# Pair products inside groups of eight fields moved to a layout with the batch in the rows, in a DLRM interaction kernel

## Chip, cores and metric

One core of one Trainium2 chip. The metric is the time of one execution on the device in microseconds (us); lower is better. All data are 32-bit floats.

## What is computed

The reference, cut to what matters: 32 fields are looked up in 32 tables, one row of 64 numbers each for 1024 examples. For each of the 496 pairs of fields i < j a number comes out of a 64x64 matrix of that pair, and these numbers with 16 dense features go through three layers.

```python
e = stack([tbl_0[ids[:, 0]], ..., tbl_31[ids[:, 31]]], axis=1)     # 1024 x 32 x 64
iu, ju = triu_indices(32, k=1)                                     # 496 pairs
z = einsum('bpe,fpe,bpf->bp', e[:, iu], kernel, e[:, ju])
h = concatenate([z, dense_ctx], axis=1)                            # 512 columns
h = maximum(h @ W_top1 + b_top1, 0)                                # 512
h = maximum(h @ W_top2 + b_top2, 0)                                # 256
y = h @ W_top3                                                     # 1
```

## The kernel before

The batch goes through in four quarters of 256 examples (QB). Two fields make a pack, 16 packs k = 0..15. Everything is written out by hand, an instruction stream per engine with counting semaphores between them.

- **Gather** (POOL, L173): per pack and quarter four indirect DMAs bring the rows of two fields for twice 128 examples into `raw`, examples in the partitions. `raw` holds 16 packs; a place is free once its pack is transposed.
- **Pack** (`transpose_pack`, L307, and `copy_x`, L192): two transposes on TensorE put a pack into `prep_ps` with the 2 x 64 features in the partitions and 256 examples in the columns, and ScalarE copies it to `xt`. `prep_ps` is a single buffer.
- **Unit** (`transform`, L278 to L299, and `multiply`, L240 to L261): a pack k is multiplied with two earlier packs m, m+1, which is eight pairs of fields. TensorE runs four matmuls of 64 rows, 128 columns of weights and 256 examples, two at a time (L289 on rows 0 to 63, L290 on rows 64 to 127), into one of three places of `t_ps`. VectorE multiplies the 1024 columns with pack k (L252) into `prod`. For odd k one unit of the row is a special one (L295, L297; on VectorE L256, L258, L260). There are 64 units a quarter. `t_ps` has three places, so a unit waits until VectorE has read the one three before it (`take_turn`).
- **Feature sums** (`feature_sums`, L321 and L324): the sum over the 64 features of a pair is a matmul too, with 32 columns of a 0/1 selector as weights and 512 columns of products, four of them side by side in `z_ps`. A burst is four units, and the sums of a burst follow the units of the next one. There are 16 bursts and so 16 rounds of sums a quarter. L329 adds the 16 dense features to free rows of `z_ps`.
- **Layers** (`copy_z`, L199; `layer`, L343, L352, L358; `copy_layer`, L209, L212, L215): ScalarE copies `z_ps` twice a quarter, and the layers of a quarter run in four pieces inside bursts 2 to 5 of the next quarter, the last quarter's at the end. A piece takes a place of `t_ps` as a unit does.

The order on TensorE (L366 to L379) is, for each burst b: its four units, a piece of a layer, the first pack due for burst b+1, the sums of burst b-1, the other packs due. ScalarE has the same order of its copies, and each engine works strictly in its written order.

```python
for b in range(QUARTERS * NB + 1):
    ... transform(v) for the four units of b ...
    if piece_after(b): layer(*piece_after(b))
    for p in before_sums(b + 1): transpose_pack(p)
    if b: feature_sums(b - 1)
    for p in after_sums(b + 1): transpose_pack(p)
```

Of the kernel before, what the change touches and what calls it, by code (L numbers as in the profile page):

```python
# [6 lines left out]
P = 128  # L7
# [4 lines left out]
PACKS = FIELDS // 2  # L12
W = 2 * QB
ZT = 2
RAW = 16
XRING = 2 * PACKS
TRING = 3
PRING = 8
BURST = 4

UNITS = [(k, tuple(range(m, min(m + 2, k)))) for k in range(1, PACKS) for m in range(0, k, 2)]
NU = len(UNITS)
NB = NU // BURST
TILE_BURSTS = NB // ZT
PACK_COL = [P * (k * (k - 1) // 2) + EMBED * (k // 2) for k in range(PACKS + 1)]
KCOLS = PACK_COL[PACKS]


def weight_cols(k, m):

    begin = PACK_COL[k] + P * m
    return slice(begin, begin + (EMBED if m == k else P))


def burst_sums(b):

    sums = [(u, n) for u in range(b * BURST, (b + 1) * BURST) for n in range(2)]
    return sorted(sums, key=lambda un: un[1] == 1 and len(UNITS[un[0]][1]) == 1)  # L40
# [3 lines left out]
Z_SLOT = {un: (b // TILE_BURSTS, at % 4, 2 * (b % TILE_BURSTS) + at // 4)  # L44
          for b in range(NB) for at, un in enumerate(burst_sums(b))}

FREE = [Z_SLOT[u, 1] for u, (_, ms) in enumerate(UNITS) if len(ms) == 1]
FREE_GROUPS = sorted({(t, g) for t, g, _ in FREE})


def packs_due(b):

    q, at = divmod(b, NB)
    if q >= QUARTERS:
        return []
    last = UNITS[at * BURST + BURST - 1][0]
    due = [k for k in range(PACKS) if k <= last and (at == 0 or k > UNITS[at * BURST - 1][0])]
    if at == 0 and q:
        due = due[2:]
    due = [q * PACKS + k for k in due]  # L60
    if at == NB - 1 and q < QUARTERS - 1:
        due += [(q + 1) * PACKS, (q + 1) * PACKS + 1]
    return due


def before_sums(b):


    return packs_due(b)[:1] if b > NB else []


def after_sums(b):
    return packs_due(b)[len(before_sums(b)):]

PIECES = 4
PIECE_BURST = 2
# [4 lines left out]
def piece_after(b):  # L83

    q, at = divmod(b, NB)
    return (q - 1, at - PIECE_BURST) if q and 0 <= at - PIECE_BURST < PIECES else None
# [6 lines left out]

def turns():

    out = []
    for b in range(QUARTERS * NB):
        out += [("unit", b * BURST + n) for n in range(BURST)]
        if piece_after(b):
            out.append(("piece", piece_after(b)))  # L100
    return out + [("piece", (QUARTERS - 1, piece)) for piece in range(PIECES)]
# [6 lines left out]
def build(nc, ids, tables, kmat, dense, w1, b1, w2, b2, w3, sel, sel_dense, ident, y):  # L108
# [3 lines left out]
    with ctx:  # L112
# [9 lines left out]
        sel_dense_sb = sb("sel_dense_sb", [P, len(FREE_GROUPS), 32])  # L122
        w1_sb = sb("w1_sb", [P, 2 * ZT, H1])
# [4 lines left out]
        dense_sb = sb("dense_sb", [P, BATCH])  # L128
        k_sb = sb("k_sb", [P, KCOLS])
        raw = sb("raw", [P, RAW, BT, 2, EMBED])  # L130
        xt = sb("xt", [P, XRING, QB])
        prod = sb("prod", [P, PRING, 4, QB])
        zt = sb("zt", [P, ZT, W])
        h1 = sb("h1", [P, H1 // P, QB])
        h2 = sb("h2", [P, H2 // P, QB])
        y_sb = sb("y_sb", [1, BATCH])

        t_ps = ctx.enter_context(nc.psum_tensor("t_ps", [P, TRING, 4, QB], fp32))
        prep_ps = ctx.enter_context(nc.psum_tensor("prep_ps", [P, QB], fp32))
# [3 lines left out]
        k_in = [sem(f"k_in{k}") for k in range(PACKS)]  # L143
        gathered = [sem(f"gathered{s}") for s in range(RAW)]
        transposed, x_copied = sem("transposed"), sem("x_copied")
        t_done, prod_done, summed, z_copied = sem("t_done"), sem("prod_done"), sem("summed"), sem("z_copied")
        layer_done, layer_copied, y_stored = sem("layer_done"), sem("layer_copied"), sem("y_stored")

        block = ctx.enter_context(nc.Block())

        @block.sync
        def _(sp):
# [296 lines left out]
```

## Time and profile before

| | |
|---|---|
| median of 3 runs | 471.23 us (471.15 to 472.52) |
| the profiled execution's own time | 471.08 us |
| its span, first to last instruction | 469.3 us |
| TensorE matmuls busy | 438.2 us, 93% |
| VectorE busy | 305.6 us, 65% |
| POOL (gathers) busy | 241.9 us, 52% |
| ScalarE busy | 42.0 us, 9% |
| granted TensorE clock, mean | 0.996 |

How it is read: busy is the time in which an engine had an instruction at work, and the sum over engines is far over the span because they overlap. The span is 1.8 us shorter than the execution's own time. The same matmul counts twice in the profile, as two instructions. A line such as L289 is a line of the kernel; `t_ps<-xt,k_sb` names the output and the inputs; PEld is TensorE's weight load, which runs beside its matmuls.

### The profile page before, as it was taken

What the parts mean: (1) busy time and instruction counts of PE and PEld (TensorE: products, weight loads), DVE (VectorE), ACT (ScalarE), POOL (GpSimd) and SP (SyncE); (2) the same over time, 40 slices, a digit from 0 to 9 for tenths busy, and PEclk for the clock granted to TensorE, in tenths of its full rate; (3) what the DMA queues carried; (4) which work ended last, traced back from release to release, by engine and by line L of the source; (5) the groups of instructions that cost most, each with busy time, mean ns of one, the idle gap of its engine ahead of it and who ended that gap; (6) DMA issues with size and microseconds to landing.
All of it is one profiled execution on the core that took longest, in us unless ns stands there. A gap on an engine that the chain in (4) does not pass through costs nothing.

```text
span 469.3 us, 7916 instructions
## 1 busy us (share of the span) xinstructions
PE 438.2 (93%) x3432; PEld 263.1 (56%) x3432; DVE 305.6 (65%) x320; ACT 42.0 (9%) x101; POOL 241.9 (52%) x260
## 2 busy tenths in 40 slices
PE   0159999999999999999999999999999999999988
PEld 0036556556456765665556674565556765565646
DVE  0045878788774656788777456788787437878850
ACT  1000000100111110000011110000001110000002
POOL 5777777777777777777777777753300000000000
PEclk9998999999999999999999999999999999999999
DMA  4444454511111111111111111110000000000000
GB/s 125 110 114 135 134 168 154 162 28 27 27 27 28 27 27 29 27 26 30 27 30 25 27 29 27 27 22 13 11 3 0 1 1 0 1 1 1 0 1 0
DMA packets 11834, 19.41 MB, mean 41 GB/s; under 512 B 5141, under 2 KB 5785, under 8 KB 11673
## 3 DMA queue, kind: packets, MB, share of 16 engines
q0 software_dynamic: 8192, 8.40, 10.1%
q1 hardware_dynamic: 2592, 8.34, 5.6%
q10 hardware_dynamic: 1016, 2.17, 1.3%
q8 instruction: 27, 0.44, 0.4%
q14 instruction: 7, 0.05, 0.0%
HBM read 18.89 MB, written 0.00 MB: 40 GB/s over the span
## 4 chain that ended last, share of the span: by engine, by line
PE 91%; POOL 5%; issue 2%; DMA 1%; DVE 1%; ACT 0%; DVEq 0%
PE t_ps L289 46%; PE z_ps L321 23%; PE t_ps L343 6%; POOL raw L173 5%; PE prep_ps L307 4%; PE t_ps L295 3%; PE t_ps L352 3%; PE t_ps L290 1%; PE z_ps L324 1%; PE t_ps L358 1%; DVE prod L252 1%; DMA raw<-tbl,ids_sb 1%; PE z_ps L329 1%; DMA ids_sb<-ids 1%; ACT xt L192 0%
## 5 line engine op out<-in xcount | busy, mean ns | idle before, releaser
L252 DVE TENSOR_TENSOR prod<-t_ps,xt 128x1024 f32<-128x1024 f32 x224 | 259.1, 1215 | 93.1 <-PE t_ps L290 93.1
L173 POOL DMA_INDIRECT raw<-tbl,ids_sb x256 | 241.7, 944 | 93.7 <-issue 76.2
L289 PE MATMUL t_ps<-xt,k_sb 64*128 64x256 f32 x960 | 232.4, 390 | 0.0
L290 PE MATMUL t_ps<-xt,k_sb 64*128 64x256 f32 x960 | 232.4, 390 | 0.0
L289 PEld LDWEIGHTS t_ps<-xt,k_sb 64*128 64x128 f32 x960 | 172.3, 188 | 67.7 <-issue 26.6
L290 PEld LDWEIGHTS t_ps<-xt,k_sb 64*128 64x128 f32 x960 | 172.4, 189 | 0.0
L321 PE MATMUL z_ps<-prod,sel_sb 128*32 128x512 f32 x960 | 122.9, 599 | 0.5 <-DVE prod L260 0.5
L321 PEld LDWEIGHTS z_ps<-prod,sel_sb 128*32 128x32 f32 x960 | 26.3, 109 | 54.7 <-issue 46.5
L256 DVE TENSOR_TENSOR prod<-t_ps,xt 128x512 f32<-128x512 f32 x32 | 21.9, 685 | 53.2 <-PE t_ps L297 53.2
L307 PE MATMUL prep_ps<-ident_sb,raw 128*128 128x128 f32 x128 | 28.5, 305 | 27.8 <-DMA raw<-tbl,ids_sb 26.7
L192 ACT ACTIVATE xt<-prep_ps 128x256 f32<-128x256 f32 x64 | 24.5, 382 | 284.6 <-PE prep_ps L307 283.3
L307 PEld LDWEIGHTS prep_ps<-ident_sb,raw 128*128 128x128 f32 x128 | 13.9, 144 | 55.1 <-issue 35.9
L343 PE MATMUL t_ps<-zt,w_sb 128*128 128x256 f32 x128 | 29.5, 385 | 0.8 <-ACT zt L199 0.8
L343 PEld LDWEIGHTS t_ps<-zt,w_sb 128*128 128x128 f32 x128 | 23.8, 190 | 6.6 <-DVE prod L252 2.4
L295 PE MATMUL t_ps<-xt,k_sb 64*64 64x256 f32 x64 | 21.1, 410 | 0.0
L297 PE MATMUL t_ps<-xt,k_sb 64*64 64x256 f32 x64 | 21.0, 410 | 0.0
L324 PE MATMUL z_ps<-prod,sel_sb 128*32 128x256 f32 x64 | 16.7, 379 | 0.0
L352 PE MATMUL t_ps<-h,w_sb 128*128 128x256 f32 x64 | 14.8, 384 | 0.0
L258 DVE TENSOR_TENSOR prod<-t_ps,xt 64x256 f32<-64x256 f32 x32 | 13.7, 427 | 0.4
L260 DVE TENSOR_TENSOR prod<-t_ps,xt 64x256 f32<-64x256 f32 x32 | 13.3, 417 | 0.4
L352 PEld LDWEIGHTS t_ps<-h,w_sb 128*128 128x128 f32 x64 | 11.9, 190 | 2.6 <-DVE prod L252 1.1
L209 ACT ACTIVATE h<-t_ps,b_sb 128x256 f32<-128x256 f32 x16 | 7.6, 473 | 57.2 <-PE t_ps L343 57.2
(15 smaller groups left out, 42.0 us busy)
## 6 DMA issues: line engine op xcount, KB each, us to landing
raw<-tbl,ids_sb POOLq DMA_INDIRECT x256, 2.5
w_sb<-w ACTq DMA_DIRECT2D x1, 1024.0 KB
k_sb<-kmat SPq DMA_DIRECT2D x1, 992.0 KB, 5.0
k_sb<-kmat SPq DMA_DIRECT2D x1, 896.0 KB
k_sb<-kmat SPq DMA_DIRECT2D x1, 864.0 KB, 4.5
k_sb<-kmat SPq DMA_DIRECT2D x1, 768.0 KB, 4.2
k_sb<-kmat SPq DMA_DIRECT2D x1, 736.0 KB, 4.0
k_sb<-kmat SPq DMA_DIRECT2D x1, 640.0 KB, 3.9
```

The costliest lines, as they stand in the source:

```text
L173: nc.gpsimd.indirect_dma_start(raw[:, p % RAW, t, f, :], None, tables[2 * k + f], bass.IndirectOffsetOnAxis(ap=ids_sb[:, q * BT + t, 2 * k ...
L192: nc.scalar.activation(xt[:, p % XRING, :], prep_ps[:], ACT.Copy).then_inc(x_copied, 1)
L252: nc.vector.tensor_tensor(prod[:, own], t_ps[:, slot], xt[:, here:here + 1, :].broadcast_to([P, 4, QB]), ALU.mult).then_inc(prod_done, 1)
L256: nc.vector.tensor_tensor(prod[:, own, 0:4:2, :], t_ps[:, slot, 0:4:2, :], xt[:, here:here + 1, :].broadcast_to([P, 2, QB]), ALU.mult)
L289: nc.tensor.matmul(t_ps[:, slot, i, :], k_sb[0:EMBED, cols], xt[0:EMBED, x, :], start=True, stop=True)
L290: last = nc.tensor.matmul(t_ps[:, slot, 2 + i, :], k_sb[EMBED:P, cols], xt[EMBED:P, x, :], start=True, stop=True)
L295: nc.tensor.matmul(t_ps[EMBED:P, slot, 1, :], k_sb[0:EMBED, cols], xt[0:EMBED, xa, :], start=True, stop=True)
L307: last = nc.tensor.transpose(prep_ps[:, t * P:(t + 1) * P], raw[:, p % RAW, t, :, :], ident_sb[:])
L321: last = nc.tensor.matmul(z_ps[rows, :], weights, prod[:, own, 2 * n:2 * n + 2, :], start=(pos == 0), stop=(pos == 15 and (tile, group) no ...
L324: last = nc.tensor.matmul(z_ps[rows, 0:QB], weights, prod[:, own, 2, :], start=False, stop=False)
L343: last = nc.tensor.matmul(t_ps[:, slot, 2 * n, :], w1_sb[:, t, m * P:(m + 1) * P], zt[:, t // 2, t % 2 * QB:(t % 2 + 1) * QB], start=(t == ...
L352: last = nc.tensor.matmul(t_ps[:, slot, 2 * n, :], w2_sb[:, t, n * P:(n + 1) * P], h1[:, t, :], start=(t == 0), stop=(t == H1 // P - 1))
```

## The change

The 16 packs are put into four groups g of four packs (eight fields). Pairs of fields from different groups stay as they are: F units, now 48 a quarter, 12 rounds of four. The 28 pairs inside a group go another way, in B units: the transposed features of a pack are now the weights and the 64x64 matrices move (`batch_transform`), so that the product has 128 examples in the partitions and the features in the columns. VectorE multiplies it with the gathered rows in `raw` as they lie (`batch_multiply`, two instructions), and ScalarE sums each pair's 64 columns with one activation that has an accumulator output (`sum_along`). A group takes four B units: two halves t of 128 examples, and for each a part 0 of 16 pairs and a part 1 of 12 pairs. So there are 64 units a quarter as before, 48 F and 16 B.

- ScalarE gets 28 activations of 128x64 per group and half, 896 in all. Their results lie in `zb`, example by row; two transposes a quarter (`turn_sums`) and a copy (`copy_turned`) turn them into the fourth part of the first layer's input. The dense features are loaded straight into `zb`, and L329 with its weights is gone.
- The order: in quarter 0 the B units stand in rounds 0, 2, 3, 6, 7 and 11; in quarters 1 and 2 a group's four stand ahead of the four F units of every third round (eight units in a row); in quarter 3 two B units stand among the four F units of rounds 0 to 7.
- From the second quarter on, packs are transposed two at a time into a `prep_ps` of 512 columns, and copied with one activation. From quarter 2 on a pair is made one round earlier.
- `raw` holds six groups, free once the group's last B unit is multiplied; `prod_a` holds six B units.
- In the last quarter three of the four parts of the first layer run ahead of the last feature sums (`last_layers`).

The numbers of rounds below run on over the quarters (12 is the first of quarter 1). Its core:

```diff
+F_UNITS = [(k, (m, m + 1)) for k in range(GROUP, PACKS) for m in range(0, k // GROUP * GROUP, 2)]
+B_UNITS = [(g, t, part) for g in range(GROUPS) for t in range(BT) for part in range(2)]
+def batch_units(r):
+    q, at = divmod(r, ROUNDS)
+    if q == 0:
+        begin = {0: (0, 4), 2: (4, 6), 3: (6, 8), 6: (8, 10), 7: (10, 12), 11: (12, 16)}.get(at, (0, 0))
+    elif q < QUARTERS - 1:
+        begin = (NBU // GROUPS * (at // 3), NBU // GROUPS * (at // 3 + (at % 3 == 0)))
+    else:
+        begin = (min(NBU, 2 * at), min(NBU, 2 * at + 2))
+    return [("B", q, u) for u in range(*begin)]
+def sums_after(r):
+    if r < EARLY_ROUNDS:
+        return []
+    if r < ROUNDS:
+        return [(0, u) for u in {10: (), 11: (12, 13)}.get(r, (r + 2,))]
+    own = [(q, u) for kind, q, u in ORDER[r] if kind == "B"]
+    return [(0, 14), (0, 15)] + own if r == ROUNDS else own
+def fills_due(r):
+    return [j for j, packs in enumerate(FILLS)
+            if FIRST_ROUND[j] - (packs[0] >= 2 * PACKS) == r and r >= EARLY_ROUNDS]
+def before_sums(r):
+    return fills_due(r)[:1] if r > 4 else []
+def after_sums(r):
+    return fills_due(r)[len(before_sums(r)):]
...
+            def sum_along(q, u):
+                g, t, part = B_UNITS[u]
+                own = nth(q, u) % ARING
+                act.wait_ge(prod_done, COUNT["B", q, u])
+                col = g * GROUP_SUMS + part * 2 * SUMS[0]
+                for n in range(2):
+                    for f in range(SUMS[part]):
+                        cells = prod_a[:, own, n, f * EMBED:(f + 1) * EMBED]
+                        last = nc.scalar.activation(cells, cells, ACT.Copy, accum_out=zb[:, q, t, col:col + 1])
+                        col += 1
+                last.then_inc(reduced, 1)
...
+            for r in range(LAST):
+                if r < EARLY_ROUNDS:
+                    for unit in ORDER[r]:
+                        for j in fills_before(unit):
+                            copy_fill(j)
+                            if j >= GROUP:
+                                sum_along(0, j - GROUP)
+                if piece_after(r):
+                    copy_layer(*piece_after(r))
+                if turn_after(r) is not None:
+                    copy_turned(turn_after(r))
+                for j in before_sums(r + 1):
+                    copy_fill(j)
+                if r and r % ROUNDS in (0, WHOLE):
+                    copy_z(*((r // ROUNDS, 0) if r % ROUNDS else (r // ROUNDS - 1, 1)))
+                for j in after_sums(r + 1):
+                    copy_fill(j)
+                if r == ROUNDS // 2:
                     load_weights()
+                for q, u in sums_after(r):
+                    sum_along(q, u)
...
+            def batch_multiply(q, u):
...
+                if nth(q, u) >= ARING:
+                    dve.wait_ge(reduced, nth(q, u) - ARING + 1)
+                dve.wait_ge(t_done, COUNT["B", q, u])
...
+                if part == 0:
+                    against_first(0, 2 * EMBED)
+                    against_first(2 * EMBED, 6 * EMBED).then_inc(prod_done, 1)
...
+            def batch_transform(q, u):
+                g, t, part = B_UNITS[u]
+                product = t_ps[:, take_turn(TURN_OF["B", q, u])].rearrange("p (n h) w -> p n (h w)", n=2)
+                pe.wait_ge(prep_copied, pack_copied(q, GROUP * g + GROUP - 1))
...
+                if part == 0:
+                    for pack, begin in ((1, 0), (3, 2 * EMBED)):
+                        for n in range(2):
+                            last = against_first(n, pack, begin)
+                else:
+                    for n in range(2):
+                        against_first(n, 2, 0)
+                    for c in range(2):
+                        for n in range(2):
+                            last = within(n, c)
+                last.then_inc(t_done, 1)
...
+            for r in range(LAST):
+                for unit in ORDER[r]:
...
+                if piece_after(r):
+                    layer(*piece_after(r))
+                if turn_after(r) is not None:
+                    turn_sums(turn_after(r))
+                for j in before_sums(r + 1):
+                    transpose_fill(j)
...
+                if r:
+                    feature_sums(r - 1)
+                for j in after_sums(r + 1):
+                    transpose_fill(j)
+            last_layers(QUARTERS - 1)
```

In `batch_transform` the 64-row matmuls move 128 and 384 columns (part 0) or 256 and twice 64 columns (part 1), each on either half of the rows. On VectorE part 0 is an instruction of 2 x 128 and one of 2 x 384 columns, part 1 one of 2 x 256 and one of 4 x 64.

## Rows read from the trace of the kernel before

**Rows 1.** The page: busy time of each engine, and TensorE's in 40 slices.

```profile
PE 438.2 (93%) x3432; PEld 263.1 (56%) x3432; DVE 305.6 (65%) x320; ACT 42.0 (9%) x101; POOL 241.9 (52%) x260
...
PE   0159999999999999999999999999999999999988
```

**Rows 2.** The page's chain that ended last, shares by line.

```profile
PE t_ps L289 46%; PE z_ps L321 23%; PE t_ps L343 6%; POOL raw L173 5%; PE prep_ps L307 4%; PE t_ps L295 3%; PE t_ps L352 3%; PE t_ps L290 1%; PE z_ps L324 1%; PE t_ps L358 1%; DVE prod L252 1%; DMA raw<-tbl,ids_sb 1%; PE z_ps L329 1%; DMA ids_sb<-ids 1%; ACT xt L192 0%
```

**Rows 3.** Stretches of the span, columns in the first line.

```profile
core 0: us, PE busy (x) PEld busy (x) DVE busy (x) ACT busy (x) POOL busy (x), PEclk, DMA share, GB/s
...
36.00:41.00 5.00, 5.00 (x33) 4.11 (x32) 2.60 (x3) 0.38 (x1) 3.78 (x5) 0.67 0.54 151
...
135.30:243.60 108.30, 108.30 (x859) 65.19 (x859) 76.31 (x81) 10.11 (x25) 81.80 (x88) 1.00 0.16 27
...
352.00:454.80 102.80, 102.23 (x816) 61.60 (x815) 71.19 (x73) 8.18 (x20) 0.00 (x0) 1.00 0.00 1
```

**Rows 4.** Timeline of TensorE's matmuls: start us, length us, line, operation.

```profile
201.19 0.48 PE L289 MATMUL t_ps<-xt,k_sb 64*128 64x256 f32 x1
...
204.85 1.92 PE L321 MATMUL z_ps<-prod,sel_sb 128*32 128x512 f32 x16
206.70 0.48 PE L289 MATMUL t_ps<-xt,k_sb 64*128 64x256 f32 x1
...
210.36 0.44 PE L307 MATMUL prep_ps<-ident_sb,raw 128*128 128x128 f32 x2
210.72 1.50 PE L321 MATMUL z_ps<-prod,sel_sb 128*32 128x512 f32 x12
```

**Rows 5.** Timeline of VectorE in the same stretch.

```profile
202.44 4.62 DVE L252 TENSOR_TENSOR prod<-t_ps,xt 128x1024 f32<-128x1024 f32 x4 [1.22 <-PE t_ps L290]
```

**Rows 6.** Timeline of TensorE at the sums that place the dense features.

```profile
303.13 0.60 PE L329 MATMUL z_ps<-dense_sb,sel_dense_sb 128*32 128x256 f32 x4
303.66 0.48 PE L289 MATMUL t_ps<-xt,k_sb 64*128 64x256 f32 x1
```

**Rows 7.** Groups by line and shape: busy us, mean ns of one, idle before.

```profile
L252 DVE TENSOR_TENSOR prod<-t_ps,xt 128x1024 f32<-128x1024 f32 x224 | 259.1, 1215 | 93.1 <-PE t_ps L290 93.1
...
L192 ACT ACTIVATE xt<-prep_ps 128x256 f32<-128x256 f32 x64 | 24.5, 382 | 284.6 <-PE prep_ps L307 283.3 <-ACT y_sb L215 1.3
...
L256 DVE TENSOR_TENSOR prod<-t_ps,xt 128x512 f32<-128x512 f32 x32 | 21.9, 685 | 53.2 <-PE t_ps L297 53.2
...
L258 DVE TENSOR_TENSOR prod<-t_ps,xt 64x256 f32<-64x256 f32 x32 | 13.7, 427 | 0.4
...
L199 ACT ACTIVATE zt<-z_ps 128x512 f32<-128x512 f32 x8 | 4.8, 597 | 36.6 <-PE z_ps L329 36.6
```

**Rows 8.** Timeline of the weight loads at a unit's start.

```profile
201.19 0.18 PEld L289 LDWEIGHTS t_ps<-xt,k_sb 64*128 64x128 f32 x1 [0.83 <-issue]
...
201.30 0.19 PEld L289 LDWEIGHTS t_ps<-xt,k_sb 64*128 64x128 f32 x1
```

**Rows 9.** Timeline of the start: the transposes of packs 0 and 3.

```profile
9.80 0.66 PE L307 MATMUL prep_ps<-ident_sb,raw 128*128 128x128 f32 x2 [9.80 <-DMA raw<-tbl,ids_sb]
...
24.80 0.69 PE L307 MATMUL prep_ps<-ident_sb,raw 128*128 128x128 f32 x2 [4.51 <-DMA raw<-tbl,ids_sb]
```

**Rows 10.** The chain of waits in order of time.

```profile
47.59 1.85 PE z_ps L321 x16
...
155.13 3.65 PE t_ps L343 x16
```

**Rows 11.** Timeline of TensorE at the last feature sums.

```profile
452.83 1.49 PE L321 MATMUL z_ps<-prod,sel_sb 128*32 128x512 f32 x11 [0.53 <-DVE prod L260]
```

**Rows 12.** Timeline of ScalarE: two operations one behind the other.

```profile
149.30 0.47 ACT L209 ACTIVATE h<-t_ps,b_sb 128x256 f32<-128x256 f32 x1 [1.19 <-PE t_ps L343]
149.67 0.38 ACT L192 ACTIVATE xt<-prep_ps 128x256 f32<-128x256 f32 x1
```

More of the change, by code:

```diff
@@ L12 @@
 PACKS = FIELDS // 2
+GROUP = 4
+GROUPS = PACKS // GROUP
+GW = 2 * GROUP * EMBED
 W = 2 * QB
-ZT = 2
-RAW = 16
+RING = 6
 XRING = 2 * PACKS
 TRING = 3
-PRING = 8
-BURST = 4
[L23 to L34, printed above, removed]
@@ new lines, in order @@
+def order():
+    out = []
+    for r in range(LAST):
+        q, at = divmod(r, ROUNDS)
+        feature = [("F", q, at * BURST + n) for n in range(BURST)]
+        batch = batch_units(r)
+        if q == 0:
+            out.append(batch + feature)
+        else:
+            out.append([x for n in range(BURST) for x in batch[n:n + 1] + feature[n:n + 1]]
+                       if q == QUARTERS - 1 else batch + feature)
+    return out
+ORDER = order()
+COUNT = {unit: n + 1 for n, unit in enumerate(x for units in ORDER for x in units)}
@@ new lines, with newest_pack, first_round @@
+QUARTER_DONE = [max(COUNT["F", q, NF - 1], COUNT["B", q, NBU - 1]) for q in range(QUARTERS)]
+def newest_pack(unit):
+    kind, q, u = unit
+    return q * PACKS + (F_UNITS[u][0] if kind == "F" else B_UNITS[u][0] * GROUP + GROUP - 1)
+FILLS = [(p,) for p in range(PACKS)] + [(p, p + 1) for p in range(PACKS, QUARTERS * PACKS, 2)]
+FILL_OF = {p: j for j, packs in enumerate(FILLS) for p in packs}
+def first_round(j):
+    return min(r for r, units in enumerate(ORDER) for x in units if newest_pack(x) >= FILLS[j][0])
@@ L94, in turns @@
+PREP_COUNT = {use: n + 1 for n, use in enumerate(prep_uses())}
 def turns():
     out = []
[L97 to L101, printed above, removed]
+    for r, units in enumerate(ORDER):
+        out += units
+        if piece_after(r):
+            out.append(("piece",) + piece_after(r))
+    return out + [("piece", QUARTERS - 1, piece) for piece in range(PIECES)]
@@ new lines, in _ @@
+            for r in range(LAST):
+                if r < EARLY_ROUNDS:
+                    for unit in ORDER[r]:
[14 more added lines that the diff above has]
+                if r == ROUNDS // 2:
@@ L266, in _ @@
+            for r in range(LAST):
+                for kind, q, u in ORDER[r]:
+                    if kind == "F":
+                        feature_multiply(q, u, r)
+                    else:
+                        batch_multiply(q, u)
         @block.tensor
@@ L339, in layer @@
                 if piece < 2:
[L340 to L345 removed]
+                    for m in (2 * piece, 2 * piece + 1):
+                        for part in (3, 0, 1, 2):
+                            last = z_part(q, m, part)
                         last.then_inc(layer_done, 1)
```

447 lines of the change are left out of this document (260 added, 187 removed).

## The prediction

> **What bounds the kernel now.** The page first: TensorE is busy 438.2 of 469.3 us and at nine tenths in nearly every slice from the third on, VectorE 305.6 us, ScalarE 42.0 [rows 1]. The chain of waits says the same by line: the units (L289) hold 46% of the span, the feature sums (L321) 23% [rows 2]. The table by stretch shows a quarter in the steady state: 108.30 of 108.30 us of matmuls against 76.3 of VectorE and 10.1 of ScalarE [rows 3]. So a microsecond off TensorE is a microsecond off the time, as long as nobody else becomes late. The timeline gives the beat: a burst starts at 201.19, its sums at 204.85, the next burst at 206.70 [rows 4], that is 3.66 us for four units and 1.85 for a round of sums, 5.51 in all. A unit is 16 half-steps of 0.215, or 0.86 us, and starting a run after sums costs 0.2.
>
> **Sums taken off TensorE.** 64 units a quarter remain, but in 12 rounds instead of 16: sixteen times a round of sums and a start fall away, 16 x (1.85 + 0.2) = **-33.0**. The sums for the dense features go too, 0.53 a quarter [rows 6]: **-2.1**.
>
> **Transposes.** Two cost 0.36, from 210.36 to 210.72 [rows 4], a further one 0.13. In quarters 1 to 3, 48 pairs of them (17.3 us) become 24 fours of 0.62 (14.9). Four turnings of the sums add 4 x 0.36 = 1.4. At each of three quarter ends the third double pack waits for the copy of the second: 512 columns (L199) are 0.60 [rows 7], so about 0.7 x 3 = 2.1; the 1.1 of such waits before goes. Together **0**.
>
> **VectorE sets the beat in long runs.** Today four units in a row are safe: VectorE starts 1.25 after the run [rows 4, 5] and takes 4.62 / 4 = 1.155 each, so the place that unit 4 needs is free at 1.25 + 1.155 = 2.41, before TensorE asks at 2.7. A B unit is two instructions: 256 columns 0.44 and 768 columns 0.95, or 512 in 0.70 and 256 in 0.43, by the line through L256, L258 and L252 [rows 7]: 1.39 and 1.13. In a run of eight (four B, four F) the eighth unit needs the fifth's place, free at 1.25 + 5.04 + 1.16 = 7.45, against 0.1 + 7 x 0.86 = 6.1: 1.35 lost, nine times (rounds 11, and four each in quarters 1 and 2). In a run of six the sixth needs the third's, 4.93 against 4.4: 0.5 lost, twelve times. 12.2 + 6 = **+18.2**. It is hidden only if the instructions of a B unit are a quarter faster than the line says; bounds 8 and 24.
>
> **Short matmuls.** A weight load of 128 columns takes a slot of 0.11 (201.19 to 201.30 [rows 8]), so the 64-column steps of part 1 (0.054 of streaming) can't go at full pace. With 0.13, as a transpose has, part 1 is 0.43 + 4 x 0.13 = 0.95 instead of 0.86, part 0 0.91. Both stay below VectorE's 1.13 and 1.39, which hide them: **0**; without that cover 0.05 x 32 + 0.09 x 32 = 4.5 more. The Trainium skill's TensorE: Matmul & The Clock Gate (LDWEIGHTS) has columns / 1.2 ns, 107 ns for 128, and speaks against moving 64 columns; by that rule, the trace agrees.
>
> **The start.** Pack 0 is transposed at 9.80 and pack 3 at 24.80 [rows 9], 5.0 a pack, by the pace of the gathers. Rounds 0 and 1 contain 12 units, the last two of which need pack 7, 44.8; with transpose, copy, two units and a round of sums that is 49.7, and pack 8, which is put in between, makes 50.7. The kernel before had its 12 units and two rounds of sums behind it at 47.59 + 1.85 = 49.4 [rows 10]. So +1.3, one round of sums not saved yet, +2.1, and the clock: the stretch 36 to 41 was granted 0.67 [rows 3], and emptier rounds leave it low somewhat longer, +0.6. **+4.0.** Later, pack 25 is there at 9.8 + 25 x 5.0 = 135 and needed after 140: the gathers don't bind again; a place in `raw` is now freed by VectorE at a group's last B unit, at the latest in round 11 for the group that is overwritten next at about 190 us, so POOL isn't stopped. The loads of the matrices on SP's queue keep their pace, a pack behind the transposes, for nearly the same bytes: nothing.
>
> **The end.** The wait of 0.53 for VectorE ahead of the last sums [rows 11] is now filled by three parts of the layer, and the last copy is half as wide: **-0.7**.
>
> Without ScalarE this makes -33.0 - 2.1 + 0 + 18.2 + 0 + 4.0 - 0.7 = -13.6.
>
> **What ScalarE's sums hold up.** They stand in the same strict order as the pack copies, at the end of a round. In round 12 ScalarE must first copy z (10.95 for TensorE's round: 8.5 of units, 0.62, 1.85; copy done at 11.5), then do six units, 84 sums of price a. Round 13 ends at 17.1 for TensorE; round 14 needs packs 24 and 25, whose copy (0.6) is queued behind the sums. TensorE stands for 11.5 + 84a + 0.6 - 17.1 = **84a - 5.0**. In round 26 the fill of `prep_ps` waits for `copy_turned`, queued behind 56 sums: 0.5 + 56a + 0.4 - 9.5 = **56a - 8.6**. Rounds 17 and 29 need the place of a layer piece (3.65 us [rows 10]) whose relus are queued: 56a - 11.3 each; rounds 21 and 33: 56a - 12.6 each; VectorE in round 12 needs `prod_a`: 28a - 5.2. In quarter 3 28a stand against a round of 7.7.
>
> The price a isn't in the trace. The copies of 256 and 512 columns take 0.382 and 0.597 [rows 7], a fixed 0.17 and 0.84 ns a column: 64 columns are 0.054 streamed, 0.22 alone, and 0.12 where they overlap, since one operation starts 0.10 before the other's end (149.30 + 0.47 against 149.67 [rows 12]). If reading the sum out is an operation of its own (another 0.17), the two are 0.19 overlapped, 0.29 if the reading has to wait for the sum, 0.39 end to end. Bounds 0.12 and 0.39. I take **0.20**, just over the overlapped pair, which is nearest to a written-out queue of independent sums. That gives 11.8 + 2.6 + 0.4 = 14.8, and 1.6 for the clock, which falls in so long a stand (as 5 us at 0.67 cost 1.65): **+16.4**.
>
> The Trainium skill's ScalarE: Activation LUTs (What ACT_TABLE_LOAD costs) gives 186 ns + 0.833 a column with 93 of overlap, 0.146 if the accumulator is free; the copies agree (0.399 by it, 0.382 here), the price of an accumulator it does not give, and no row here shows one. By it the waits would be 7.3 + 1.6 and the whole about 466.
>
> **Sum.** 471.08 - 13.6 + 16.4 = 473.9 for the profiled execution; the median of the runs is 0.15 above it: **474.0**. About 0.3%, or 1.4 us, is what a measurement can tell from nothing, so this is slower, hardly.
>
> **Rivals.** *ScalarE dearer* (a 0.25 to 0.30, reading waits): 16.0 to 20.2, 5.4 to 8.2, and 2.7 x 2 to 5.5 x 2, VectorE 1.8 to 3.2, up to 4.2 x 2 in rounds 21 and 33, 2 to 3 of clock, 2 in quarter 3: with 31 to 55 the time is 488 to 512. For it: summing ends before it can be read. Against: the order would be poor by tens of microseconds. Chance 0.20.
> *ScalarE cheap*, the other side: a single mechanism, the queue of 84 in round 12. The waits equal the savings where 140a - 13.6 + 1.6 = 13.6, at a = 0.18. At a = 0.12 to 0.17 they are 6 to 12 and the time 463 to 470, faster. For it: overlapped operations [rows 12]. The Trainium skill's ScalarE: Activation LUTs, as cited above, would put the time here. Chance 0.26.
> *The savings come in full*: VectorE's B instructions are quicker than the line, or TensorE's B units are, and ScalarE's sums below 0.12: -35.1 + 3.3 + 8 + 5 gives 452, with neither 439. Against: the rows of VectorE fit a line well. Chance 0.12.
> *Nothing changes*, savings and waits cancel within 1.4: 0.05.
> The forecast, a from 0.18 to 0.25 and 471 to 488, has 0.37.
>
> **The numbers.** Faster: 0.26 + 0.12 = 0.38. Same: 0.05 and a slice of the forecast, 0.10. Slower: 0.52. The range leaves 0.2 outside: 450 to 506. The forecast's own is 471 to 488, the faster cases' 450 to 470.
>
> **What would show it.** TensorE's idle time before the first F unit of round 14, ended by a ScalarE copy, of 12 us, and the clock low behind it; another of 2 to 3 in round 26; runs of eight with idle steps ended by VectorE. `sum_along` rows of about 0.2 us pitch, 896 of them and ScalarE near 220 us busy. TensorE's L321 count down by a quarter. The prediction is wrong if round 14 starts without a wait, if the sums' pitch is outside 0.17 to 0.24, or if the eight-unit runs take under 7.2 us.

## The result: 483.3 us against 471.3, and the profile after

The changed kernel takes 483.3 us in the median of four runs (480.8 to 484.72), the kernel before 471.3 beside it (471.15 to 472.52). That is 12.0 us more. The ratio is 1.0243, 95% interval 1.0193 to 1.0294. So the change costs about 2.4%, well clear of the noise. The profiled execution took 480.8 us, 9.7 more than the one before, and the rows below are its own.

The page of the kernel after: busy time, the slices, and the chain that ended last.

```profile
PE 411.3 (86%) x3544; PEld 271.4 (57%) x3544; DVE 290.6 (61%) x320; ACT 252.5 (53%) x1873; POOL 242.0 (51%) x260
...
PE   0165999999972499899989789899889999999997
...
ACT  1036247363459509519850925708880886679202
...
PEclk9997799999998599999999979999999999999999
...
PE 53%; ACT 30%; POOL 6%; DVE 5%; issue 4%; DMA 1%; ACTq 0%; DVEq 0%
ACT prod_a L358 28%; PE t_ps L480 23%; PE z_ps L557 13%; POOL raw L312 6%; PE t_ps L495 5%; PE t_ps L564 5%; DVE prod_a L436 4%; PE t_ps L599 3%; PE prep_ps L528 3%; ACT xt L333 1%; DMA raw<-tbl,ids_sb 1%; PE t_ps L481 1%; PE t_ps L605 1%; PE t_ps L502 1%; DVE prod_a L447 1%
```

Against [rows 1] TensorE has 27 us less to do and the span is still longer: there is now a hole in the 13th and 14th slice (2 and 4), where ScalarE shows a 9 and then a 5, and the clock falls to 5 in the 15th. In the chain some 90% of the share was TensorE's lines [rows 2]; now ScalarE has 30%, and one line holds 28 of them, L358, the feature sums moved to ScalarE:

Groups by line and shape of the kernel after (columns as in [rows 7]).

```profile
L358 ACT ACTIVATE prod_a<-prod_a 128x64 f32<-128x64 f32 x896 | 214.0, 242 | 9.2 <-DVE prod_a L436 4.5 <-issue 3.5 <-ACT y_sb L379 1.2
L358 ACT ACTIVATION_READ_ACCUMULATOR prod_a<-prod_a 128x1 f32 x896 | 169.3, 189 | 0.0
L557 PE MATMUL z_ps<-prod,sel_sb 128*32 128x512 f32 x512 | 64.9, 617 | 0.0
L557 PE MATMUL z_ps<-prod,sel_sb 128*32 128x256 f32 x512 | 30.9, 382 | 0.0
L436 DVE TENSOR_TENSOR prod_a<-t_ps,raw 128x768 f32<-128x768 f32 x32 | 30.3, 946 | 0.0
L436 DVE TENSOR_TENSOR prod_a<-t_ps,raw 128x256 f32<-128x256 f32 x32 | 13.5, 421 | 91.0 <-PE t_ps L495 89.9 <-ACT prod_a L358 1.1
```

Each of the 896 sums is two instructions, the activation and the reading of the accumulator. The timeline shows their pitch, and what is queued behind them. ScalarE in the kernel after (start us, length us, line, operation):

```profile
141.16 0.25 ACT L358 ACTIVATE prod_a<-prod_a 128x64 f32<-128x64 f32 x1
141.31 0.19 ACT L358 ACTIVATION_READ_ACCUMULATOR prod_a<-prod_a 128x1 f32 x1
141.40 0.24 ACT L358 ACTIVATE prod_a<-prod_a 128x64 f32<-128x64 f32 x1
...
160.96 0.25 ACT L358 ACTIVATE prod_a<-prod_a 128x64 f32<-128x64 f32 x1
161.10 0.20 ACT L358 ACTIVATION_READ_ACCUMULATOR prod_a<-prod_a 128x1 f32 x1
161.20 0.58 ACT L333 ACTIVATE xt<-prep_ps 128x512 f32<-128x512 f32 x1
```

From 141.16 to 141.40 is 0.24 us a sum, each instruction starting about 0.1 before the one ahead of it ends. The queue of round 12 runs from 141.16 to 161.20, and only then comes the copy of packs 24 and 25. TensorE in the same stretch:

```profile
144.40 0.66 PE L528 MATMUL prep_ps<-ident_sb,raw 128*128 128x128 f32 x4
144.98 1.93 PE L557 MATMUL z_ps<-prod,sel_sb 128*32 128x512 f32 x16
161.93 0.76 PE L480 MATMUL t_ps<-xt,k_sb 64*128 64x256 f32 x1 [15.02 <-ACT xt L333]
```

The packs were transposed at 144.40 and their first user started at 161.93. This is the single stand of 15 us, before the F units of round 14. Behind it TensorE's matmuls are 0.63 long instead of 0.38 for 3.5 us. The table by stretch gives the granted clock there as 0.50, the lower of its two levels (1.2 GHz instead of 2.4):

```profile
161.90:165.50 3.60, 3.58 (x17) 3.12 (x19) 1.22 (x1) 0.00 (x0) 2.74 (x3) 0.50 0.17 27
```

The waits by who ended them (us in total, times, longest):

```profile
PE t_ps L480 <- ACT xt L333: 15.0, 1, 15.0
...
PE prep_ps L528 <- ACT zbt L340: 5.1, 2, 4.6
...
PE t_ps L495 <- ACT xt L333: 3.8, 3, 1.8
...
PE t_ps L480 <- ACT h L370: 3.1, 2, 1.8
```

The 4.6 is round 26, where the copy of the turned sums is queued; `xt L333` ahead of L495 are the waits before rounds 21 and 33 (1.8 and 1.5) and one of 0.5 at the start, `h L370` those of rounds 17 and 29 for a piece of the layer. By quarter the table of stretches after reads (columns as in [rows 3]):

```profile
127.60:252.95 125.35, 102.45 (x891) 68.58 (x890) 72.75 (x80) 76.82 (x580) 94.88 (x101) 0.95 0.15 28
252.95:364.00 111.05, 102.04 (x892) 66.98 (x888) 72.48 (x80) 62.22 (x466) 52.90 (x57) 0.97 0.10 18
364.00:479.00 115.00, 111.81 (x960) 74.92 (x956) 72.37 (x80) 64.23 (x471) 0.00 (x0) 1.00 0.01 2
```

A steady quarter was 108.30 [rows 3]. In the kernel before the first quarter ended at 129.5 and the last began at 346.1. So the second is 17.0 longer and the third 2.7; the first gained 1.9 and the last, with the end, 8.2. Together +9.7. The loss sits mainly in the quarter with the queue of 84 sums.

### The profile page after: what moved, and what is told of

Read it like the earlier page. It is cut to its first block, busy times and chain, and to the rows that moved or that the text cites. A ratio compares the mean times of both kernels' runs of the same rounds, so it can differ in the third digit from the quotient of the medians.

```text
span 479.0 us, 10048 instructions
## 1 busy us (share of the span) xinstructions
PE 411.3 (86%) x3544; PEld 271.4 (57%) x3544; DVE 290.6 (61%) x320; ACT 252.5 (53%) x1873; POOL 242.0 (51%) x260
## 4 chain that ended last, share of the span: by engine, by line
PE 53%; ACT 30%; POOL 6%; DVE 5%; issue 4%; DMA 1%; ACTq 0%; DVEq 0%
ACT prod_a L358 28%; PE t_ps L480 23%; PE z_ps L557 13%; POOL raw L312 6%; PE t_ps L495 5%; PE t_ps L564 5%; DVE prod_a L436 4%; PE t_ps L599 3%; PE prep_ps L528 3%; ACT xt L333 1%; DMA raw<-tbl,ids_sb 1%; PE t_ps L481 1%; PE t_ps L605 1%; PE t_ps L502 1%; DVE prod_a L447 1%
## 5 line engine op out<-in xcount | busy, mean ns | idle before, releaser
L420 DVE TENSOR_TENSOR prod<-t_ps,xt 128x1024 f32<-128x1024 f32 x192 | 222.6, 1214 | 79.7 <-PE t_ps L481 79.7
L358 ACT ACTIVATE prod_a<-prod_a 128x64 f32<-128x64 f32 x896 | 214.0, 242 | 9.2 <-DVE prod_a L436 4.5
L480 PE MATMUL t_ps<-xt,k_sb 64*128 64x256 f32 x768 | 193.7, 395 | 24.0 <-ACT xt L333 15.0
L481 PE MATMUL t_ps<-xt,k_sb 64*128 64x256 f32 x768 | 193.8, 395 | 0.0
L480 PEld LDWEIGHTS t_ps<-xt,k_sb 64*128 64x128 f32 x768 | 137.5, 190 | 72.9 <-issue 23.4
L358 ACT ACTIVATION_READ_ACCUMULATOR prod_a<-prod_a 128x1 f32 x896 | 169.3, 189 | 0.0
L481 PEld LDWEIGHTS t_ps<-xt,k_sb 64*128 64x128 f32 x768 | 137.6, 190 | 0.0
L436 DVE TENSOR_TENSOR prod_a<-t_ps,raw 128x256 f32<-128x256 f32 (+2 forms) x96 | 61.1, 682 | 92.6 <-PE t_ps L495 89.9
L557 PE MATMUL z_ps<-prod,sel_sb 128*32 128x256 f32 (+1 forms) x1024 | 95.9, 500 | 0.0
L333 ACT ACTIVATE xt<-prep_ps 128x512 f32<-128x512 f32 (+1 forms) x40 | 20.3, 508 | 107.3 <-PE prep_ps L528 107.3
L495 PE MATMUL t_ps<-k_sb,xt 64*128 64x384 f32 (+2 forms) x384 | 52.6, 400 | 3.8 <-ACT xt L333 3.8
L495 PEld LDWEIGHTS t_ps<-k_sb,xt 64*128 64x128 f32 x384 | 29.5, 191 | 25.5 <-issue 13.2
L370 ACT ACTIVATE h<-t_ps,b_sb 128x256 f32<-128x256 f32 x16 | 7.2, 470 | 34.4 <-PE t_ps L564 34.4
L502 PEld LDWEIGHTS t_ps<-k_sb,xt 64*128 64x128 f32 x256 | 20.0, 190 | 1.4
L564 PEld LDWEIGHTS t_ps<-zt,w_sb 128*128 128x128 f32 x96 | 18.2, 190 | 3.4 <-ACT zt L348 1.0
```

The costliest lines, as they stand in the source:

```text
L358: last = nc.scalar.activation(cells, cells, ACT.Copy, accum_out=zb[:, q, t, col:col + 1])
L420: nc.vector.tensor_tensor(prod[:, own], t_ps[:, slot], xt[:, here:here + 1, :].broadcast_to([P, 4, QB]), ALU.mult).then_inc(prod_done, 1)
L436: return nc.vector.tensor_tensor(out[:, :, begin:begin + width], product[:, :, begin:begin + width], rows[:, 0:width].unsqueeze(1).broadca ...
L480: nc.tensor.matmul(t_ps[:, slot, i, :], k_sb[0:EMBED, cols], xt[0:EMBED, x, :], start=True, stop=True)
L481: last = nc.tensor.matmul(t_ps[:, slot, 2 + i, :], k_sb[EMBED:P, cols], xt[EMBED:P, x, :], start=True, stop=True)
L495: return nc.tensor.matmul(product[:, n, begin:begin + cols.stop - cols.start], xt[n * EMBED:(n + 1) * EMBED, slot_of(q, GROUP * g + pack), ...
```

## The experiments

**Theories.** *Queue*: ScalarE's sums cost the time by where they stand in its order, ahead of copies that TensorE waits for. Spread out, they cost nearly nothing. *Pace*: the longer runs of units make VectorE the bound, and the sums are innocent. *Nothing gained*: taking sums off TensorE yields less than counted. The first two are told apart by moving the sums without removing them; by leaving out 6 or 4 of each unit's 8 and 6 sums, which takes the load away; and by halving VectorE's work for the batch units.

**First six runs: the same edits with the lookups as they are.** All of the four kernels are the changed kernel with one edit. Round 12's own sums moved to round 13:

```diff
-    return [(0, 14), (0, 15)] + own if r == ROUNDS else own
+    if r == ROUNDS:
+        return [(0, 14), (0, 15)]
+    if r == ROUNDS + 1:
+        return [(1, 0), (1, 1), (1, 2), (1, 3)]
+    return own
```

Only one of each part's sums computed (the rest of `zb` set to zero once; the other columns' sums are left out, 128 sums instead of 896):

```diff
-                    for f in range(SUMS[part]):
+                    for f in range(1):
```

The sums of quarters 1 and 2 spread over a group's three rounds, one unit, one unit, two units (in quarter 1 round 12 has the two old ones, 13 the first new one, 14 the other three):

```diff
-    own = [(q, u) for kind, q, u in ORDER[r] if kind == "B"]
-    return [(0, 14), (0, 15)] + own if r == ROUNDS else own
+    q, at = divmod(r, ROUNDS)
+    if q == QUARTERS - 1:
+        return [(q, u) for kind, q, u in ORDER[r] if kind == "B"]
+    if r == ROUNDS:
+        return [(0, 14), (0, 15)]
+    if r == ROUNDS + 1:
+        return [(1, 0)]
+    if r == ROUNDS + 2:
+        return [(1, 1), (1, 2), (1, 3)]
+    g, i = divmod(at, 3)
+    return [(q, 4 * g + u) for u in ((0,), (1,), (2, 3))[i]]
```

And, on top of the missing sums, only the first of a batch unit's two multiplications (the other products are left out):

```diff
-                if part == 0:
-                    against_first(0, 2 * EMBED)
-                    against_first(2 * EMBED, 6 * EMBED).then_inc(prod_done, 1)
-                else:
-                    against_first(0, 4 * EMBED)
...
+                against_first(0, (2 if part == 0 else 4) * EMBED).then_inc(prod_done, 1)
```

> Only ScalarE's order is changed: the 56 sums of round 12's own four B units come after round 13's pack copy instead of before it; the 28 sums of units 14 and 15 stay. Queue theory: the copy of packs 24 and 25 is done 1.3 us after TensorE asks for it, so of the stand of 15.0 us before round 14 and the 1.8 us of slow clock behind it some 15.5 us go: 465 to 468 us. Rival (another wait takes its place: the deferred sums now hold the turned sums or a layer piece): 475 us or more. Rival (the long runs of eight and VectorE are what costs): no change, 481 to 484 us.

> Left out: of each B unit's 16 or 12 sums only 2 are made, the other columns of zb are zero. ScalarE's 768 fewer sums are 184 us of its time. Queue theory: all waits behind ScalarE, added up from the trace as 33.5 us (15.1 and 1.8 of clock in round 14, 2.8 in round 12, 2.1 and 1.5 in rounds 17 and 29, 1.9 and 1.6 in 21 and 33, 4.7 and 2.0 of clock in 26), go, and the time is 447 to 450 us. Rival (VectorE's runs of eight and TensorE's short matmuls cost as much as ScalarE): 455 us or more. It is also the bound that any reordering of ScalarE can reach.

> All sums are made, but those of a group are spread over the three rounds after its B units (one unit, one unit, two units), each behind that round's pack copy; quarter 3 is as it was. Queue theory: no queue before a copy is longer than 28 sums or 6.7 us, less than the round that follows, so only the wait for prod_a in round 12 stays (2.8 us): 450 to 454 us. Rival (the amount of ScalarE's work, not its place in the order, is what costs): above 465 us.

> As e2_no_sums, and the second of VectorE's two instructions of each B unit is left out too, so a B unit costs VectorE 0.3 or 0.6 us and it is no longer behind in a run of eight. If VectorE sets the beat in runs of eight (0.76 us each, nine) and six (0.4 us each, twelve), 11 to 12 us under e2_no_sums, about 437 us. If it is TensorE's short matmuls that make these runs longer, the same time as e2_no_sums.

Measured: 717.4 (716.1 to 720.3), 711.6 (710.9 to 712.0), 715.9 (714.0 to 718.1) and 700.4 (699.8 to 701.9) us, and the kernel before itself 598.1 (590.6 to 599.0), not 471. On another chip the spread kernel and the one with 128 sums were run again.

> The kernel of e4_spread_sums once more, since on the chip of that run the kernel before itself took 598 us: a group's sums lie behind the pack copies of three rounds (one unit, one, two) instead of all behind one. Queue theory: the waits behind ScalarE that the trace of the changed kernel adds up to 33.5 us go, all but 2.8 for prod_a in round 12: 450 to 454 us. Rival (the amount of ScalarE's work, not its place in the order, is what costs): above 465 us.

> The kernel of e2_no_sums once more (2 sums of each B unit's 16 or 12 are made, the other columns of zb are zero). Queue theory: 447 to 450 us, 33.5 us under the changed kernel's 480.8 to 484.7. Rival (VectorE's runs of eight and TensorE's short matmuls cost as much as ScalarE): 455 us or more.

Measured: 716.9 (714.4 to 722.4) and 708.7 (708.3 to 711.7), before 595.9 (589.8 to 601.0). All six expected times missed by over 200 us. Only the step that halving VectorE's work was to bring came out, 11.2 us (711.6 to 700.4) where 11 to 12 were expected. On the queue the runs say nothing: something else of over 120 us, present in the unchanged kernel too, covers it. The page of the spread kernel with its lookups shows where the time goes.

```profile
PE   0400002009789196657859586683929999999998
...
POOL 6777777700531605470620707043260000000000
```

TensorE is nearly empty through POOL's first long busy stretch, then works, then is empty again in places. TensorE's timeline of the same kernel puts a number to it:

```profile
120.77 0.76 PE L489 MATMUL t_ps<-xt,k_sb 64*128 64x256 f32 x1 [87.02 <-issue]
...
160.72 0.76 PE L489 MATMUL t_ps<-xt,k_sb 64*128 64x256 f32 x1 [35.55 <-issue]
```

and POOL's the break between:

```profile
142.50 0.94 POOL L321 DMA_INDIRECT raw<-tbl,ids_sb  x1 [0.30 <-issue]
...
186.33 0.94 POOL L321 DMA_INDIRECT raw<-tbl,ids_sb  x1 [42.89 <-DVE prod_a L456]
```

POOL issued its last indirect DMA before a full ring at 142.50, and TensorE stood until 160.72 with nothing to wait for that the profile shows ("issue"). It is not TensorE alone. ScalarE, in the middle of one unit's sums, here starts an instruction about every 1.4 us instead of every 0.12:

```profile
125.15 0.26 ACT L367 ACTIVATE prod_a<-prod_a 128x64 f32<-128x64 f32 x1 [1.20 <-issue]
126.55 0.20 ACT L367 ACTIVATION_READ_ACCUMULATOR prod_a<-prod_a 128x1 f32 x1 [1.14 <-issue]
```

In the first profiles the same 256 indirect DMAs were issued and no such hole stands. With a ring of 24 packs instead of 16 POOL issues longer in one go, which fits that the changed kernels suffer more (717 against 598); that wasn't tried alone, and the changed kernel itself was not run with its lookups on these chips.

**Six runs with plain lookups.** To test the theories apart from this, the 256 indirect DMAs were replaced, in the kernel after, in the kernel before and in the edited ones, by plain DMAs of as many bytes from fixed rows, issued from SP, a pack's four once the pack before has landed, with the loads of the matrices on the same queue between them (the lookup by ids is left out, so the output is another one; the work of all other engines is the same):

```diff
-                        nc.gpsimd.indirect_dma_start(
-                            raw[:, n % RING, t, begin:begin + EMBED], None, tables[2 * k + f],
-                            bass.IndirectOffsetOnAxis(ap=ids_sb[:, q * BT + t, 2 * k + f:2 * k + f + 1], axis=0),
-                        ).then_inc(gathered[n % RING * GROUP + at], 16)
+                        sp.dma_start(raw[:, n % RING, t, begin:begin + EMBED], tables[2 * k + f][0:P, :]
+                                     ).then_inc(gathered[n % RING * GROUP + at], 16)
```

(cut to its core). The comparison is now between the kernels of this setting. After, spread and 128 sums ran on one chip, before, two a round and half of VectorE's work on another.

> The changed kernel with one part replaced: the lookups are left out. Each of the 256 indirect DMAs is a plain DMA of the first 128 rows of its table, issued from SP, a pack's four DMAs once the pack before has landed; POOL does nothing. All work of TensorE, VectorE and ScalarE and its order is as in the changed kernel. It is the base for the next kernels, on chips on which the indirect DMAs keep the other engines from their instructions (the kernel before takes 596 to 598 us there). If POOL's issuing is what holds them up, the time comes near the changed kernel's first profile, 470 to 485 us, with the wait of about 15 us before round 14. Otherwise it stays above 590 us.

> The kernel before with the same replacement as in h1_after_plain: the lookups are left out, each of the 256 indirect DMAs is a plain DMA of the first 128 rows of its table from SP, a pack's four once the pack before has landed. It says what the change and its repair are worth side by side. The packs come every 4.1 us instead of 5.0 (round 2 of h1_after_plain starts 10.6 us earlier than in the changed kernel), of which the kernel before can use what lies before its fourth pack and a little more: 462 to 466 us. So the change costs 4 to 8 us (h1_after_plain at 469.6) and with its sums spread it gains 22 to 27 us (h2_spread_plain at 439.2). If the change were no gain even with ScalarE out of the way, this kernel would be under 440 us.

Measured: after 469.6 (468.2 to 469.7), before 458.6 (458.2 to 459.1), on chips on which the kernel before with its indirect DMAs took 600.0 and 595.5. So the holes go with the indirect DMAs issued from POOL; whether by their kind, their queue or their pace, all three of which were changed, isn't shown. Without them the change costs 11.0 us, against 12.0 by the first medians and 9.7 by the first profiles. The kernel before came out 3 to 7 us lower than expected, and with it missed what was expected of the change (a cost of 4 to 8 us) and of the spread (a gain of 22 to 27). All of it lies at the start: its first feature sums begin at 29.3 us instead of 41.2 in the first profile, and behind them every round takes the same time to 0.01 us, though the chips differ. The stand is there unchanged in the kernel after with plain lookups, in TensorE's timeline:

```profile
151.34 0.76 PE L483 MATMUL t_ps<-xt,k_sb 64*128 64x256 f32 x1 [15.01 <-ACT xt L336]
```

Now the three edits of the sums. "Two a round" is the changed kernel with the batch units themselves two a round through quarters 1 and 2, each behind a feature unit, as quarter 3 has them; their sums follow:

```diff
-    elif q < QUARTERS - 1:
-        begin = (NBU // GROUPS * (at // 3), NBU // GROUPS * (at // 3 + (at % 3 == 0)))
...
-                       if q == QUARTERS - 1 else batch + feature)
+                       if q else batch + feature)
```

> As h1_after_plain, and a group's sums lie behind the pack copies of three rounds (one unit, one, two). Queue theory: about 30 us under h1_after_plain (the waits of rounds 14, 17, 21, 26, 29, 33 and the clock behind them). Rival (the amount of ScalarE's work, not its place in the order): less than 10 us under it.

> As h1_after_plain, and of each B unit's 16 or 12 sums only 2 are made (the other columns of zb are zero). Queue theory: 33 us under h1_after_plain, and no more than 4 us under h2_spread_plain. Rival (VectorE's runs of eight and short matmuls are the larger cost): less than 15 us under h1_after_plain.

> As h1_after_plain, and only the place of the B units in quarters 1 and 2 is changed: two in each of a quarter's first eight rounds, among the F units, as quarter 3 has them, instead of a group's four in a row at every third round; ScalarE sums them at the end of their own round, two units or 28 sums (6.7 us) a round. Queue theory: only round 12 still has a long queue (units 14 and 15 and two of its own, 56 sums, 13.4 us against a round of 8.2 that follows): a wait of about 6 us before round 14, 1 to 2 more later, instead of 34 in all: 442 to 447 us. VectorE's pace gives nothing, eight runs of eight (0.76 each) become sixteen of six (0.36). Rival (the row of eight itself is harmful beyond the queue): under 438 us. Rival (the amount of sums): above 460 us.

> As h3_no_sums_plain (431.4), and the second of VectorE's two instructions of each B unit is left out too. If VectorE sets the beat in the runs of eight (7.85 us against the 7.1 that TensorE's pace would give, nine of them) and of six (5.7 against 5.4, twelve), 10 to 11 us under it: 420 to 422 us. If TensorE's short matmuls lengthen the runs, the same time as h3_no_sums_plain.

Measured:

| kernel, plain lookups | us (lowest to highest) | against after |
|---|---|---|
| before | 458.57 (458.22 to 459.09) | -11.0 |
| after | 469.56 (468.23 to 469.70) | 0 |
| after, sums spread | 439.23 (437.49 to 440.83) | -30.3 |
| after, batch units two a round | 442.55 (442.05 to 444.34) | -27.0 |
| after, 128 of 896 sums | 431.43 (430.64 to 431.75) | -38.1 |
| the same, half of VectorE's B work | 421.32 (420.99 to 421.70) | -48.2 |

The spread kernel decides it: it does every sum, on the same engine, and is 30.3 us faster. Its page, and two rows of its waits:

```profile
PE 407.3 (93%) x3544; PEld 270.1 (62%) x3544; DVE 290.6 (66%) x320; ACT 253.5 (58%) x1873; POOL 0.2 (0%) x4
...
PE   0379999999978999999999999999999999999997
...
ACT  1167355562459854668576644676597964889003
```

```profile
PE t_ps L492 <- ACT xt L345: 1.7, 1, 1.7
...
DVE prod_a L448 <- ACT prod_a L370: 2.6, 2, 1.6
```

ScalarE is as busy as in the kernel after (253.5 against 252.5), TensorE's wait in front of round 14 went from 15.0 to 1.7, and the hole in the slices is gone. So the queue theory holds: 30.3 of the 38.1 us that 768 of the sums cost come from their place, not their number. *Nothing gained* falls too: without the queue the change is 19.3 us (4.2%) faster than the kernel before.

What is left of the sums' cost is the 7.8 us from the spread kernel to the one with 128 sums. At most 4 had been expected, and 38.1 instead of 33 for leaving the sums out. Comparing the two round by round: 3.7 at the start, where the sums of units 0 to 3 stand ahead of pack copies, 2.8 in round 12, where VectorE waits for a place in `prod_a` and TensorE for VectorE, 1.7 before round 14, 0.4 in round 36; 8.6 in all, against 8.7 between the spans of the two profiles (438.6 and 429.9). The profiled execution of the spread kernel (440.45) was granted a clock of only 0.61 from 34.9 to 39.6 us. Of its other runs one has the same mean clock of 0.992 and took 440.8, the two at 1.000 took 437.5 and 438.0. So some 2 to 3 us of the 7.8 come and go with the clock.

Two a round came out within its expectation, with the one wait it was to have, in its list of waits:

```profile
PE t_ps L480 <- ACT xt L333: 5.2, 1, 5.2
```

The pace theory holds for 10.1 us, the difference of the last two kernels, measured with the sums out of the way. With them in place it was not tried. Taken off the 11.0 it would leave about 1, so that the change would be slower without the pace isn't shown; without the queue the change is faster in spite of it.

## Why the prediction was right, and where its sum was off

**Direction, range and mechanism** hold: slower, inside 450 to 506, by a queue of sums on ScalarE ahead of a copy in round 14. The point was 474.0, the median is 483.3. The 9.3 us between are two larger errors of opposite sign, and that they nearly cancel is luck: with ScalarE's term alone as measured the forecast would have been 496, with the others alone about 461, on the other side.

| term | predicted | shown |
|---|---|---|
| sums and starts off TensorE, dense sums, transposes, end | -35.8 | about -41 (what is left) |
| VectorE's pace | +18.2 | +10.1 |
| the start, without ScalarE's part | +4.0 | +4.3 |
| what ScalarE's sums hold up | +16.4 | +38.1 |
| sum | +2.8 | +11.0 plain, +9.7 with lookups |

The second and fourth rows are differences of two kernels. The third goes by the kernels with plain lookups: 12 units and the first sums are through at 39.7 with 128 sums (a round of 2.05 still unsaved), 12 units and two rounds of sums at 37.4 in the kernel before. The first is what is left for the 11.0 to come out. (Its -33.0 for the sums is 16 x 2.05 = 32.8; and 16 steps of 0.215 make four units, a unit has four.) **It can be seen directly**, in the stretches of the kernel with 128 sums and plain lookups, a steady quarter in each row:

```profile
113.30:214.25 100.95, 100.02 (x892) 66.84 (x891) 72.42 (x80) 20.57 (x100) 0.00 (x0) 1.00 0.17 37
214.25:315.30 101.05, 99.64 (x890) 66.33 (x886) 72.42 (x80) 17.50 (x82) 0.00 (x0) 1.00 0.05 12
```

A quarter of 101.0 has four runs of eight, which lose 0.70 to 0.76 each (below), and with half of VectorE's work it takes 98.0, against 108.30 - 8.25 - 0.53 = 99.5 by the prediction. The 1.5 a quarter more wasn't counted because the prediction took all of the kernel before's bursts for 3.66 us [rows 4]. Its bursts with a short unit (L295) are longer, as TensorE's timeline of the kernel before shows at the place behind [rows 4]:

```profile
213.21 0.43 PE L295 MATMUL t_ps<-xt,k_sb 64*64 64x256 f32 x1
...
216.66 0.64 PE L321 MATMUL z_ps<-prod,sel_sb 128*32 128x512 f32 x4
```

From the sums at 210.72 [rows 4] to those at 216.66 are 5.94 us, not 5.51. The change has no such units. There were eight a quarter; at 0.43 they would give 3.4, so something takes some 2 of it back. What, was not tried.

**VectorE sets the beat in long runs: right in kind, too dear.** The term that failed is the 1.39 + 1.13 for the two parts of a B unit. VectorE in the kernel after:

```profile
116.64 1.89 DVE L436 TENSOR_TENSOR prod_a<-t_ps,raw 128x256 f32<-128x256 f32 x3 [0.91 <-PE t_ps L495]
118.44 0.41 DVE L447 TENSOR_TENSOR prod_a<-t_ps,raw 128x256 f32<-128x256 f32 x1
118.77 1.87 DVE L436 TENSOR_TENSOR prod_a<-t_ps,raw 128x256 f32<-128x256 f32 x3
120.56 0.41 DVE L447 TENSOR_TENSOR prod_a<-t_ps,raw 128x256 f32<-128x256 f32 x1
120.90 1.21 DVE L420 TENSOR_TENSOR prod<-t_ps,xt 128x1024 f32<-128x1024 f32 x1
```

The lengths are as forecast (0.42, 0.95, 0.68, 0.41 by the groups), but from 116.64 to 120.90, where the next instruction starts, four units take 4.26 us, 1.07 each, not 1.26: each instruction starts about 0.08 before the one ahead has ended. The prediction had seen that of ScalarE [rows 12] and added up whole durations on VectorE. The rows of before held it for VectorE too: four of 1.215 each [rows 7] take 4.62 in a row [rows 5], not 4.86. A run of eight takes 7.85 us against 7.1 unhindered, so up to 0.76 lost instead of 1.35, a run of six about 0.36 instead of 0.5; 9 x 0.76 + 12 x 0.36 = 11.2, and 10.1 were measured.

**What ScalarE's sums hold up: the formula right, its price and its list short.** The price of a sum was taken as 0.20 and is 0.24, between the "overlapped" 0.19 and the "reading waits" 0.29. With it the formula gives for the stand before round 14 84 x 0.24 - 5.0 = 15.2, and 15.0 were measured; for round 26 4.8 against 4.6. All the formulas of the prediction at 0.24, with the 1.6 of clock, give 29.1, which would have made the forecast about 487. The way in which the two follow each other was right, both overlapped: the reading starts 0.10 before the activation ends, and the next activation 0.10 before the reading does. What was short were the lengths, 0.242 and 0.189 where 0.22 and 0.17 had been worked out from copies, since no row of before has an activation with a reading behind it. The Trainium skill's ScalarE: Activation LUTs (What ACT_TABLE_LOAD costs) gives 186 ns + 0.833 a column less 93 of overlap, from which an estimate for the activation alone is 0.146. The trace agrees for that half: the reading starts 0.15 behind it. But the reading adds 0.09, which the page doesn't price, and at 0.146 the prediction's sum gives 466, under the time of before.

TensorE's timeline of the kernel after shows round 26, its sums at nearly half their pace behind the stand:

```profile
277.45 1.11 PE L528 MATMUL prep_ps<-ident_sb,raw 128*128 128x128 f32 x4 [4.59 <-ACT zbt L340]
278.50 3.45 PE L557 MATMUL z_ps<-prod,sel_sb 128*32 128x512 f32 x16
```

Most of the other 9 us of ScalarE's 38.1 come from places that the list did not have: 3.7 at the start (the sums of quarter 0 before pack copies), a second fall of the clock, behind the stand in round 26 (1.65 to 2.0 us), two waits of 0.8 at quarter ends, and some 1.3 more in round 12 than 28a - 5.2 says. Rounds 21 and 33 lose 1.8 more than 56a - 12.6 gives. The signs it named were there, but larger: 12 us before round 14 were 15.0, 2 to 3 in round 26 were 4.6, and ScalarE is 252.5 us busy, not near 220. So the total confirms no single term: 21.7 too little on ScalarE and 13 too much on the rest cancelled in part.

**Costed at nothing, and so it was:** the matmuls of 64 columns. TensorE in the kernel after, the four B units of round 12 and the first F unit behind them:

```profile
127.61 1.57 PE L495 MATMUL t_ps<-k_sb,xt 64*128 64x128 f32 x12
129.01 0.56 PE L502 MATMUL t_ps<-k_sb,xt 64*128 64x64 f32 x8
129.41 1.52 PE L495 MATMUL t_ps<-k_sb,xt 64*128 64x128 f32 x12
...
131.15 0.47 PE L480 MATMUL t_ps<-xt,k_sb 64*128 64x256 f32 x1
```

From 127.61 to 131.15 the four take 3.54 us, less than the 3.66 of F units, though the 64-column steps go at 0.10 us (four of them, two matmuls side by side, from 129.01 to 129.41) and not at the 0.054 of streaming. The Trainium skill's TensorE: Matmul & The Clock Gate (LDWEIGHTS) has the number of columns / 1.2 ns for a weight load, which is 107 ns for 128, and the step agrees with that. Behind the start the gathers and SP's queue showed no new wait in the first profile. At the end the wait of 0.53 for VectorE is gone and the one for the last copy is 0.51 instead of 0.82.

**The rivals.** *ScalarE cheap* needed a pitch under 0.18 and has 0.24. *ScalarE dearer* (0.25 to 0.30) was nearly met in its price, and met for its waits (31 to 55; 33.5 in the first profile by adding its waits and clock losses), but its mechanism, a reading that waits, is not what the rows show, and its 488 is missed since the rest of the sum was 10 us better. *The savings in full* (452) needed sums below 0.12 and a quick VectorE; it had 0.24, and 10.1 us lost to the pace. The spread kernel reaches a gain of that size (19.3 us) at the same prices, by another order.

**Open.** Why TensorE stood for "issue" beside POOL's indirect DMAs (seen in the profiles of two later chips, and by the times on all four) and not in the first profiles, for the unchanged kernel too, no run here tells. The spread kernel, 4.2% under the kernel before with plain lookups, could only be timed with its real lookups where this covered everything (716.9 us), so what it brings with them elsewhere isn't shown.

## What to carry to other kernels

Work moved to an idle engine costs what stands behind it in that engine's order, not its share of busy time: here 768 sums, over 180 us of ScalarE, cost 7.8 us when spread, and 20 us of them in one queue ahead of a copy cost 15 and a fall of the clock. Write, for each moved step, the wait it makes as a line in its unknown price (84a - 5), do so for every consumer of that engine, the start's and the quarter ends' too, and see at which price the sign turns. When the lengths of instructions are added up for an engine's pace, take the distance from start to start; where only lengths are known, allow for an overlap.

## What the runs showed that was not expected

A sum by an activation with an accumulator is two instructions, 0.24 and 0.19 us long, at a pitch of 0.24 us for 64 columns. VectorE instructions back to back cost about 0.08 us less each than their lengths, large ones (4.62 for four of 1.215) as well as small. The granted clock fell not only behind the stand of 15 us but also behind one of 4.6. And on four chips kernels with indirect DMAs issued back to back from POOL took 120 us and more longer, with stands of TensorE of up to 87 us for nothing that the profile names and ScalarE at about 1.4 us an instruction; with plain DMAs of the same bytes from SP these were gone (on one chip, the kernel before took 595.5 with the one kind and 458.6 with the other).
